# A conditioned-mix and LoRA kernel: x of tile 1 loaded behind W, the third block of W transposed ahead of tile 0, the rounded products in front of the remainder, tile 1 in 512 columns

## The reference, cut to what matters

```python
x = x + einsum('bct,bcd->bdt', x, W0[cond])          # W0: (16, 32, 32)
base  = einsum('bsi,oi->bso', x, W)                  # W: (512, 512)
low   = einsum('bsi,bir->bsr', x, lora_A[label])     # lora_A: (5, 512, 32)
delta = einsum('bsr,or->bso', low, lora_B) * 0.5     # lora_B: (512, 32)
x = x + base + delta
```

## Time and profile before

| What | Value |
|---|---|
| median of 3 runs | 75.79 us (75.51, 75.79, 79.14) |
| the profiled execution, device time | 74.88 us |
| its span | 73.1 us |
| TensorE matmuls busy | 69.3 us (95% of the span) |
| TensorE weight loads busy | 55.7 us (76%) |
| VectorE, ScalarE, GpSimd busy | 41.7, 34.9, 32.2 us |
| mean granted TensorE clock | 1.00 |

### The profile page before, as it was taken

The page is one execution under the profiler, slowest core; times in us unless marked ns, Lnnn a source line. Parts: engine busy times, 40 slices in busy tenths (PEclk is TensorE's granted clock), DMA queues, the critical chain, the costliest instruction groups (busy, mean ns, idle before and its releaser), DMA issues.

```text
span 73.1 us, 2439 instructions
## 1 busy us (share of the span) xinstructions
PE 69.3 (95%) x1006; PEld 55.7 (76%) x1006; DVE 41.7 (57%) x64; ACT 34.9 (48%) x83; POOL 32.2 (44%) x75
## 2 busy tenths in 40 slices
PE   4999999999999999999999999999999999999950
PEld 3788999987786768888687588888876788858930
DVE  4018769999489799919972669439016190213220
ACT  1536667699033974729702452834915538004100
POOL 4652678699980047878932058867000100000000
PEclk9999999999999999999999999999999999999999
DMA  0989999345397650048965000059910000599694
GB/s 7 328 259 372 226 238 205 63 134 151 101 211 263 182 127 13 9 95 196 283 174 158 9 4 17 19 137 181 247 36 9 0 0 0 117 192 264 186 241 158
DMA packets 11727, 10.25 MB, mean 140 GB/s; under 512 B 1092, under 2 KB 9028, under 8 KB 11716
## 3 DMA queue, kind: packets, MB, share of 16 engines
q1 hardware_dynamic: 11200, 9.83, 53.2%
q0 software_dynamic: 512, 0.26, 1.9%
q10 hardware_dynamic: 4, 0.00, 0.0%
HBM read 5.90 MB, written 4.19 MB: 138 GB/s over the span
## 4 chain that ended last, share of the span: by engine, by line
PE 95%; DVE 1%; issue 0%
PE p_u L642 18%; PE p_u L643 17%; PE p_u L644 17%; PE p_low L624 7%; PE p_y L653 5%; PE p_u L648 4%; PE p_low L709 4%; PE p_y L686 4%; PE p_fold L633 3%; PE p_y L642 3%; PE p_y L644 3%; PE p_y L643 3%; PE p_y L678 1%; PE p_low L695 1%; PE p_fold L695 1%; PE p_low L644 1%
## 5 line engine op out<-in xcount | busy, mean ns | idle before, releaser
L642 PE MATMUL p_u<-m_hi,xt_hi 128*128 128x512 f32 (+2 forms) x66 | 24.1, 364 | 0.0
L643 PE MATMUL p_u<-m_lo,xt_hi 128*128 128x512 f32 (+2 forms) x66 | 23.3, 354 | 0.0
L644 PE MATMUL p_u<-m_hi,xt_lo 128*128 128x512 f32 (+2 forms) x66 | 23.3, 354 | 0.0
L291 POOL DMA_INDIRECT w_sel<-in_L_cond_weights,w_row x16 | 16.9, 1057 | 12.3 <-PE p_y L653 8.0
L642 PEld LDWEIGHTS p_u<-m_hi,xt_hi 128*128 128x128 f32 x66 | 12.5, 189 | 2.2 <-issue 0.6
L644 PEld LDWEIGHTS p_u<-m_hi,xt_lo 128*128 128x128 f32 x66 | 12.5, 189 | 1.8
L643 PEld LDWEIGHTS p_u<-m_lo,xt_hi 128*128 128x128 f32 x66 | 12.5, 189 | 1.6
L469 DVE STREAM_TRANSPOSE xt<-x_sb 128x512 f32<-128x512 f32 x12 | 13.0, 1105 | 0.1
L498 DVE COPY u_sb<-p_u 128x512 f32<-128x512 f32 x6 | 4.2, 692 | 12.4 <-PE p_u L648 10.1
L370 ACT ACTIVATE xt_hi<-xt 128x512 fp32r<-128x512 f32 x12 | 6.9, 627 | 7.3 <-PE p_u L648 5.1
L492 DVE TENSOR_TENSOR xt_lo<-xt,xt_hi 128x512 fp32r<-128x512 f32 x12 | 8.4, 732 | 0.2
(11 more groups left out here) (80 smaller groups left out, 80.2 us busy)
## 6 DMA issues: line engine op xcount, KB each, us to landing
x_sb<-in_x SPq DMA_DIRECT2D x24, 128.0 KB
out<-y_sb SPq DMA_DIRECT2D x12, 256.0 KB
w_sb<-in_L_cond_W SPq DMA_DIRECT2D x4, 256.0 KB, 4.1
x_rows<-in_x SPq DMA_DIRECT2D x2, 256.0 KB, 3.5
x_rows<-in_x SPq DMA_DIRECT2D x1, 512.0 KB, 5.0
out<-y_two SPq DMA_DIRECT2D x4, 128.0 KB
a_sb<-in_L_cond_lora_A SPq DMA_DIRECT2D x1, 320.0 KB
w_sel<-in_L_cond_weights,w_row POOLq DMA_INDIRECT x16, 4.0
```

Of the source, the lines that this page charges most:

```text
L291: nc.gpsimd.indirect_dma_start(out=w0_sel[:, t, :], out_offset=None, in_=W0_rows, in_offset=bass.IndirectOffsetOnAxis(ap=w0_row[:, t:t + 1 ...
L642: mm(to, xt_hi[:, slot, c, rows], m_hi[:, c, cols], start=(c == 0 and first), stop=False)
L643: mm(to, xt_hi[:, slot, c, rows], m_lo[:, c, cols], start=False, stop=False)
L644: mm(to, xt_lo[:, slot, c, rows], m_hi[:, c, cols], start=False, stop=False)
```

## The change

SyncE issues the load of x of tile 1 behind all four blocks of W in place of between the second and the third. TensorE transposes the third block of W (k = 2) directly behind the second; then come the eight products of tile 0 with `m_hi` in the left 256 columns, the fourth block, the four products with `m_lo`, the transposes of tile 1, and the same eight and four products in the right 256 columns. Tile 1 is made in one go in 512 columns, and B is transposed behind it. ScalarE and VectorE split all four blocks of M ahead of tile 1.

```diff
             sp.dma_start(x_rows[:, 0], x_tile[0]).then_inc(s_rows_in[0], 16)
-            for o in W_ORDER[:2]:
+            for o in W_ORDER:
                 sp.dma_start(w_sb[:, o], W[P * o:P * (o + 1), :]).then_inc(s_w_in[o], 16)
             sp.dma_start(x_rows[:, 1], x_tile[1]).then_inc(s_rows_in[1], 16)
-            for o in W_ORDER[2:]:
-                sp.dma_start(w_sb[:, o], W[P * o:P * (o + 1), :]).then_inc(s_w_in[o], 16)
...
             split_m(1)
-            split_rows(1, p_fold)
             split_m(2)
             split_m(3)
+            split_rows(1, p_fold)
...
+            def main_rounded(bank, u, cols, first):
+                rows = slice(P * u, P * (u + 1))
+                for c in range(C):
+                    mm(bank[:, cols], xt_hi[:, 0, c, rows], m_hi[:, c, cols], start=(c == 0 and first), stop=False)
+                for c in range(C):
+                    mm(bank[:, cols], xt_lo[:, 0, c, rows], m_hi[:, c, cols], start=False, stop=False)
+
+            def main_remainder(bank, u, cols):
+                rows = slice(P * u, P * (u + 1))
+                for c in range(C):
+                    mm(bank[:, cols], xt_hi[:, 0, c, rows], m_lo[:, c, cols], start=False, stop=False)
...
             transpose_w(1)
-            transpose_rows(1, p_fold)
-
-            block = [slice(P * o, P * (o + 1)) for o in W_ORDER]
-            pe.wait_ge(s_xlo, 1)
-            pe.wait_ge(s_mlo, 1)
-            main_tile(p_u[0], 0, 0, block[0], chunks=(0, 1))
             pe.wait_ge(s_diag_pool, 2)
             transpose_w(2)
-            pe.wait_ge(s_mlo, 2)
-            main_tile(p_u[0], 0, 0, block[1], first=False, chunks=(0, 1))
+
+            pe.wait_ge(s_xlo, 1)
+            pe.wait_ge(s_mhi, 2)
+            main_rounded(p_u[0], 0, left, True)
             pe.wait_ge(s_diag_pool, 3)
             transpose_w(3)
-            main_tile(p_u[0], 0, 0, left, chunks=(2, 3))
+            pe.wait_ge(s_mlo, 2)
+            main_remainder(p_u[0], 0, left)
+            transpose_rows(1, p_fold)
+            pe.wait_ge(s_mhi, 4)
+            main_rounded(p_u[0], 0, right, False)
+            pe.wait_ge(s_mlo, 4)
+            main_remainder(p_u[0], 0, right)
             pe.wait_ge(s_xlo, 2)
             pe.wait_ge(s_cond_sb, 1)
-            main_tile(p_u[1], 0, 1, left)
-            pe.wait_ge(s_mlo, 4)
-            main_tile(p_u[0], 0, 0, right, first=False)
+            main_tile(p_u[1], 0, 1)
             transpose_b(p_y[0])
-            main_tile(p_u[1], 0, 1, right, first=False)
             pe.wait_ge(s_xlo, 3)
             main_tile(p_y[2], 1, 0)
```

## The result

The changed kernel took 79.39 us (median of six runs, 75.99 to 82.32) where the kernel before took 75.88 (75.21 to 79.14). On another chip six more runs gave a median of 80.02 (77.52 to 80.27) against 75.32, a ratio of the medians of 1.062. The ratio of 1.020 alone leaves open whether the loss reaches two per cent; with all six runs of the second chip at 77.5 or more against a median of 75.32, the change is slower, and both medians lie outside the forecast's 75.2 to 76.9.

What follows compares the result with a forecast made beforehand. TensorE's own matmul time plus small holes was taken as the bound. Work saved and old waits removed, against new holes and a later `copy_low`, summed to about +0.3 us: median 76.1 us, range 75.2 to 76.9.

Steps and rivals of the forecast that it cites:

- The gain in work, 0.74 us: At the start, fewer and wider matmuls for tiles 0 and 1 would save 0.61 and 0.13 us, together 0.74.
- Third block: Its load would land at 6.52, its transposes start at 7.18 instead of 7.89, behind a 0.75 us hole from 6.43.
- my early bound: Landing earlier, the third block could gain at most 0.22 us, since TensorE sees the second block's `m_hi` at about 7.43.
- The hole ahead of tile 1 and tile 2's own wait: TensorE would wait 0.21 us from 11.71 for tile 1's `xt_lo`; tile 2's `xt_lo` would be in time by 0.4.
- The wait of 0.09 for GpSimd ahead of `low_group`: This old wait would go, because GpSimd gets its fourth block 0.9 us earlier: 0.09 us saved.
- B's new place, 0.28: B's later transposes delay VectorE by 1.30 us against 1.05 of slack, so `copy_low` and `spread_low` come 0.28 us later.
- Past 20.35 the order is unchanged and TensorE has no cushion to give it back: Behind the start of `spread_low` nothing more would change, so the loss of about 0.3 us would stay to the end.
- SyncE issues the same transfers in the same number: Among the moves that cost nothing: B and all loads behind it would land as before.
- Rival (c), the clock: Idleness around the third block's hole at the start drops the matmul clock, costing 2.3 us: 78.4 us; chance 0.06.
- Rivals (a): Third block lands early (-0.22) and VectorE's delay stays under its slack (-0.28): 75.6 us, or 75.4; chance 0.2.
- (b): Third block still lands at 7.19, the first hole is 1.42 and everything 0.67 us later: 76.8 us; chance 0.1.
- The aside that ends in "about 0.25": By the skill's 81 ns per narrow matmul, the first part of the work gain would be about 0.25 us, not 0.61.

Runs made afterwards that it cites:

- after_again: The changed kernel run once more, unaltered, on another chip: median 80.02 us against 75.32 for the kernel before.
- a_hole18: The changed kernel with 18 tiny matmuls added, nine ahead of the third block's transposes and nine behind: 75.94 us, ratio 1.011 to the kernel before.
- a_hole18_b: a_hole18 with B transposed ahead of tile 1 as well: 75.16 us, ratio 0.995 to the kernel before.
- a_rows_late: The changed kernel with the 512 KB load of the last two tiles' rows put behind pair 5's loads: 76.67 us, ratio 1.017 to the kernel before.
- a_pad18: The changed kernel with 18 matmuls more: four warm-up products in place of six, plus 20 tiny ones; 77.04 us, ratio 1.006 to the kernel before.
- after: The changed kernel itself, as first measured and profiled: median 79.39 us, ratio 1.020 to the kernel before; profiled execution 80.28 us.
- a_b_early: The changed kernel with B transposed ahead of tile 1 and `bw_rep` moved up on ScalarE: 78.86 us, ratio 1.032 to the kernel before.
- b_minus17: The kernel before with 17 matmuls fewer in about the same time, 512-column stand-ins replacing most products of tiles 0 and 1: 77.59 us, ratio 1.033.
- a_pad18_oldload: a_pad18 with the load of x of tile 1 put back between W's second and third block: 78.80 us, ratio 1.018 to the kernel before.
- a_warm24: The changed kernel with its six warm-up products of 512 columns replaced by 24 of 128: 78.03 us, ratio 1.042 to the kernel before.

## Why the prediction was wrong

- **What bounds the kernel**: right that only matmul time and holes count. I took "issue 0%" of the chain as a property of the kernel. It was a property of when the program's pieces arrived.
- **The gain in work, 0.74 us**: the costs were right. Eight rounded products took 9.08 - 8.05 = 1.03 (1.04), tile 1 took 14.98 - 12.11 = 2.87 (2.83).
- **Third block**: it landed at about 6.2, earlier than 6.52, and gained nothing. `m_hi` was then the last, as in my early bound, but at 8.05 in place of 7.43: the second block came 0.2 later, and its four transposes took 1.13 us where the earlier trace rows has 0.75, so that ScalarE could start only at 7.31. The eight transposes start 0.21 us apart until about 7.1 and 0.12 behind that; before, they were 0.12 apart from 6.2 on. The array reached its upper level a microsecond or more later in this execution, with 1.00 in the column of the granted clock, and the sum had nothing for it. (The step is real, but my 0.49 for a warm-up product was a mean duration; from start to start it is 0.43 against the 0.229.)
- **The hole ahead of tile 1 and tile 2's own wait**: 11.71 + 0.21 became 12.11; tile 2 followed B without a wait. Right. The wait of 0.09 for GpSimd ahead of `low_group`, which I had going, stayed: 18.28 against 17.96 + 0.23.
- **B's new place, 0.28**: right in mechanism and size (2.40 against 2.15 us from `low_group` to `spread_low`); `copy_low` started at 19.94 with no slack. The changed kernel stood at +0.61 there, I had said +0.28.
- **"Past 20.35 the order is unchanged and TensorE has no cushion to give it back"**: the step that failed. The order was unchanged, the supply of the program was not. I counted 18 matmuls fewer as a pure gain; they moved each program request by 18 matmuls in time, into a burst of loads, and the sum had no term for it. In the profiled execution it cost 2.77 us and, by the clock behind it, 1.23. "SyncE issues the same transfers in the same number" also held for the data only.
- **Rival (c), the clock**: the mechanism exists and I gave it 0.06. In the profiled execution it struck behind the standstill; in after_again at the start, where I had placed it, and not behind the standstill. But the longer wait there is set by the landing of W, which varied from 5.3 to about 6.8 us for the second block, and the kernel before can show it too. How much of it the new order adds stays open: a_hole18 had 2 high runs of 11, a_hole18_b 5 of 12, the kernel before 2 of 23 above 76.9 in the same rounds.
- **Rivals (a) and (b)** were questions of half a microsecond and lay inside the range. The aside that ends in "about 0.25" gives 0.32 by the working behind its 0.02; the sum does not use it. No rival had a resource that the rows of before didn't show as a wait.

Open as well: how much of a packet's lateness is a late request and how much late service. The first is shown by the count, the second by moving one load; their shares of the 5.2 us I can't separate, beyond the wait of at least 3.3 us that a_rows_late gives. And 0.77 us behind the last matmul: the four stores of `y_two` are issued in 3.44 us in the changed kernel and in a_rows_late, 2.70 in a_pad18 and 2.71 before, with a program packet of 1.6 us beside them instead of 0.9. That was seen and not tested.

## What to carry to other kernels

In a fully unrolled kernel whose TensorE is the bound, list the instruction packets in the DMA view before and after every edit, and check where dense stretches of tiny matmuls (here 128 in 1.3 us; all four standstills lay in one, which no run tests by itself) cross the next piece of program while loads are in flight. A saving in the number of instructions early on moves all later crossings; if time appears as "issue" in the middle of a group, pad by the number you removed and look again before judging the edit. Read the trace of more than one execution when the runs of a kernel spread by 6 us.

## What the runs showed of the hardware

- TensorE's program came in eight packets of 16 KB, each about 0.9 to 1.7 us on one DMA engine, and a late one stopped the engine for 1.45 to 2.80 us with no semaphore in the profile (after, a_b_early, after_again, b_minus17). TensorE went on 1.3 to 1.5 us behind the packet's end.
- After 2.41 us of standstill (after) and 2.80 (a_b_early) the granted clock went to 0.50 (1.2 GHz) for about 3 us, in the second case only about 1 us behind the restart; after 2.05 us (after_again) and 1.45 (b_minus17) it stayed at 1.00.
- The step from 1.2 to 2.4 GHz at the start came between 4.4 us (after_again, four transposes at 4.44 in 0.75) and 13.8 us (a_pad18_oldload), and the granted clock read 1.00 in both; the duration of like groups is the better sign. At the lower level a product of 128 columns took 0.21 us from start to start (a_warm24) and one of 512 took 0.43 (before).
